# Gated linear attention levels: one head per row tile in two banks, both halves of a level in one step, q without zeros, and the third output copy ahead of the exponent

## The chip, the cores and the metric

The kernel runs on one core of one Trainium2 chip. The metric is the time of one execution on the device in microseconds. The kernel before takes 1231.93 us (median of three runs, 1231.51 to 1234.69).

## The reference, cut to what matters

The input is 16 sequences of 512 tokens with 256 features, all fp32. Each goes through a layer norm, gated linear attention, a second layer norm and a residual, then a layer norm, a two-layer feed-forward block with the weights of one of eight experts (two sequences share an expert), another layer norm and a residual. The attention has 4 heads with 64 key and 128 value features:

```python
def step(S, inp):
    qt, kt, vt, gt = inp
    S = jnp.exp(gt)[:, None] * S + kt[:, None] * vt[None, :]
    return (S, qt @ S)
...
q = (x @ Wq) ... * scale;  k = (x @ Wk);  v = (x @ Wv)
g = log_sigmoid(x @ gk_w1 @ gk_w2 + gk_b) / 16.0
o = scan(step)                                    # over 512 tokens, per head
o = o * rsqrt(mean(o * o) + EPS) * rms_w
o = o.reshape(b, t, DV) * silu(x @ Wg)
return o @ Wo
...
h = gelu(tokens @ w1[e] + b1[e]);  y = h @ w2[e] + b2[e]
```

## The kernel before, in words

The scan is done in chunks of 128 tokens. Inside a chunk the matrix of q times k with all decays between the two tokens is built in seven levels with half block sizes h = 1, 2, 4, ..., 64 (`LV`). At level i the tokens of the second half of each block of 2h tokens are multiplied with the keys of its first half; then q of the second halves is multiplied by the product of the gates of the first halves, and k of the first halves by that of the second halves (`q_update` on VectorE, L631; `k_update` on GpSimd, L1142). After seven levels q and k carry the decay to the chunk's ends, as the state needs it.

Features lie on partitions: 256 key features are two tiles (`tl`) of 128 partitions, with two heads each. q is stored block-diagonally in `qbd` (L65): [128, tl, head of the tile, 512 tokens], with zeros where the partitions belong to the other head, so that one matmul over 128 rows gives both heads side by side. A half level (`level(i, tl)`, L283) issues, for the levels 0 to 4 (`MASKED`), 16 fp32 matmuls in blocks of 32 tokens: 32 keys stationary, 2 x 16 q columns moving, the output in one of four strips of 32 partitions of bank `PL[tl]`. The compiler makes two passes (a weight load and a matmul each) of an fp32 matmul. VectorE copies the valid places by mask to `AC` (`copy_pairs`, L610). Levels 5 and 6 use blocks of 32 and 64 keys, and ScalarE copies their outputs to `Am` (`copy_blocks`, L899). The diagonal comes from `diag_rows` and `diag_columns`; `expand` (L911) puts the 32-token blocks into `Am`.

All engines run an order written out by hand in a function `run(s, j, e, B, C, A)`, called once per step. In a step of the main loop, part B is the levels and attention of sequence s, part C the feed-forward of sequence s - 1, part A the start of sequence s + 1 (layer norm, gates, k and q projections; v and output gate projections too). j is 1 for odd s. The loop has 14 steps with A, B and C; before it stand a step with A alone and one with A and B, after it one with B and C and one with C.

The level stage is a loop over 14 half levels, `step` = 2i + tl, on every engine. TensorE issues a half level and then one slice of other work (L509 to L525): `f1(m)`, six untiled matmuls of 512 columns for one of eight feature tiles of the first feed-forward layer, or `f2(c)`, 24 of 256 columns. ScalarE makes the GELU and the high part `h_hi` of each f1 slice and VectorE the low part `h_lo`. Each level waits for the q update, the k update and the copies of the level before (L294 to L300). With j = 1, GpSimd also makes the low parts of W2 in the level stage (`weight_lo`, L1175); with j = 0, ScalarE makes the high part of the next W1 at step 11 (`weight_hi`, L891, L983) and GpSimd its four low parts from step 12 on, the last two between the `rsqrt(3, c)` that end the feed-forward's layer norm.

Then comes the middle stage: x transposes, `kh` (keys to tokens), the gate matmuls `gd` and `gl`, `kp`, `qp`, `vp`, `gp` (projections of sequence n = s + 1), and per chunk c the state `st(c)`, attention `att(c)` into the one bank `PO`, the transposes `ogt(c)` and the output projection `wo(c)` (L526 to L580). `att(c)` waits until ScalarE has copied the output of chunk c - 1 out of `PO` (`o_evac`, L919, waited for at L474). ScalarE's order around the third copy is at L1014 to L1033: `o_evac(1)`, `squares(1)`, `og_hi(0)`, `v_evac(0)`, the exponent that gives the gates (L1023, with a table load), `g_evac(0)` (Silu, with a table load), `v_evac(1)`, `o_evac(2)`. VectorE writes q times scale times gates to `qg`, which shares its memory with the gates' argument `gm` (L80); ScalarE copies it from there into the two diagonal blocks of `qbd` (`q_blocks`, L948, four copies). `S` (L75) holds the state of the two heads of a tile one above the other; `att` multiplies it head by head with `qbd`.

Of the kernel before, what the change touches and what calls it, by code (L numbers as in the profile page):

```python
# [21 lines left out]
def build(nc, x_d, wq_d, wk_d, wv_d, wg_d, w1g_d, w2g_d, gkb_d, wo_d, rms_d,  # L22
# [6 lines left out]
    P = 128  # L29
# [22 lines left out]
    with ctx:  # L52
# [12 lines left out]
        qbd = sb("q_blockdiag", [P, KT, 2, T])  # L65
# [9 lines left out]
        S = sb("state", [P, KT, HV])  # L75
# [4 lines left out]
        gm = qg = sb("gate_and_q", [P, 2, T])  # L80
# [49 lines left out]
        def totals(h):  # L130
# [11 lines left out]
            pe_drow=1, pe_diag=1, pe_lv=2 * NL, pe_kt=2, pe_st=NCH - 1, pe_att=NCH, pe_ogt=NCH, pe_wo=NCH,  # L142
# [7 lines left out]
            dv_c0=KT, dv_cp=2 * MASKED, dv_qu=2 * NL, dv_st=2 * (NCH - 1) - 1, dv_og=NCH * H,  # L150
# [6 lines left out]
            ac_xhi=KT, ac_gr=1, ac_abs=KT, ac_e=1, ac_l=1, ac_a=1, ac_k=KT, ac_v=NCH, ac_g=NCH, ac_qb=2 * KT,  # L157
# [6 lines left out]
            po_p1=1, po_p2=NCH, po_p3=NCH, po_p4=NCH, po_x2=NCH, po_fin=NCH, po_tot=NL, po_ku=2 * NL,  # L164
# [14 lines left out]
        def states(c):  # L179
            return max(2 * c - 1, 0)  # L180
# [78 lines left out]
        def _(pe):  # L259
# [19 lines left out]
            def run(s, j, e, B, C, A):  # L279
# [3 lines left out]
                def level(i, tl):  # L283
                    h = LV[i]
                    if i == 0:
                        if tl == 0:
                            pe.wait_ge(sem["ac_qb"], at("ac_qb", s, 2 * KT))
                            pe.wait_ge(sem["dv_q"], at("dv_q", s, 2 * KT))
                            if C:
                                pe.wait_ge(sem["ac_o"], at("ac_o", p, NCH))  # L290
                            pe.wait_ge(sem["ac_k"], at("ac_k", s, KT))
                        if C:
                            pe.wait_ge(sem["dv_t"], at("dv_t", p, 3 + tl))
                    else:  # L294
                        pe.wait_ge(sem["dv_qu"], at("dv_qu", s, 2 * (i - 1) + tl + 1))
                        pe.wait_ge(sem["po_ku"], at("po_ku", s, 2 * (i - 1) + tl + 1))
                        if i - 1 < MASKED:
                            pe.wait_ge(sem["dv_cp"], at("dv_cp", s, 2 * (i - 1) + tl + 1))
                        else:
                            pe.wait_ge(sem["ac_cp"], at("ac_cp", s, 4 * (tl + 1)))  # L300
                    for c in range(NCH):
                        if i < MASKED:
                            for g in range(CH // BS):
                                t = slice(c * CH + BS * g, c * CH + BS * (g + 1))
                                q = qbd[:, tl, :, t].rearrange("p a (n t h) -> p a n t h", t=2, h=h)
                                last = nc.tensor.matmul(PL[tl][BS * g:BS * (g + 1), c * BS:(c + 1) * BS],  # L306
                                                        kk[:, tl, t], q[:, :, :, 1, :], start=True, stop=True)
                            continue
                        for b in range(HC // h):
                            g = h * (c % 2) + 64 * b  # L310
                            t = c * CH + 2 * h * b
                            last = nc.tensor.matmul(PL[tl][g:g + h, (c // 2) * 2 * h:(c // 2 + 1) * 2 * h],  # L312
                                                    kk[:, tl, t:t + h], qbd[:, tl, :, t + h:t + 2 * h],
                                                    start=True, stop=True)
                    last.then_inc(sem["pe_lv"], 1)

                def diag_rows():

                    for tl in range(KT):
# [40 lines left out]
                def kh(f):  # L360
                    pe.wait_ge(sem["po_ku"], at("po_ku", s, 2 * NL))
# [106 lines left out]
                def att(c):  # L468
                    pe.wait_ge(sem["ac_ex"], at("ac_ex", s, 4 * KT))
                    pe.wait_ge(sem["ac_cp"], at("ac_cp", s, 12))  # L470
                    pe.wait_ge(sem["dv_qu"], at("dv_qu", s, 2 * NL))
# [4 lines left out]
                    for hd in range(H):  # L476
                        tl, hh = hd // 2, hd % 2
                        w = slice(hd * HV, (hd + 1) * HV)
                        last = nc.tensor.matmul(PO[:, w], Am[:, tl, 2 * c + hh, :], v[:, c, w],  # L479
                                                start=True, stop=(c == 0))  # L480
                        if c:
                            last = nc.tensor.matmul(PO[:, w], qbd[:, tl, hh, c * CH:(c + 1) * CH],  # L482
                                                    S[:, tl, :], start=False, stop=True)
# [25 lines left out]
                for step in range(2 * NL):  # L509
                    if B:  # L510
                        level(step // 2, step % 2)
                        if step == 1:
                            diag_rows()
                        if step == 3:
                            diag_columns()
                        if not C and 2 <= step < 10:
                            (vp, gp)[step % 2](step // 2 - 1, s)
                    if C:
                        if step == 1:
                            x3t(0)  # L520
                            x3t(1)
# [40 lines left out]
                if V:  # L562
                    gp(1, n)
# [708 lines left out]
```

## Time and profile before

| | |
|---|---|
| median of three runs | 1231.93 us |
| profiled execution, its own time | 1233.3 us |
| its span, first to last instruction | 1231.5 us |
| PE busy | 1129.4 us (92%), 12368 matmul passes |
| PEld busy | 923.2 us (75%) |
| VectorE busy | 863.8 us (70%) |
| ScalarE busy | 813.9 us (66%) |
| GpSimd busy | 630.6 us (51%) |
| granted TensorE clock, mean; 29.6 to 30.7 us; 542.9 to 543.6 us | 0.979; 0.50; 1.00 |
| chain that ended last | PE 62%, ACT 21%, DVE 9%, issue 7% |

PE is TensorE's matmuls, PEld its weight loads, which overlap them; DVE, ACT and POOL are VectorE, ScalarE and GpSimd. An end of a matmul is modelled, so the start times say more than the lengths. In a timeline a line merges neighbouring instructions of one form, with their count, and in square brackets stands the idle time of the engine before it and who ended it. A form as `128*32 128x32` is stationary rows by columns, then the output's partitions by columns.

### The profile page before, as it was taken

How to read it: one execution, taken by the hardware profiler on the slowest of the kernel's cores; microseconds unless marked ns; L12 is line 12 of the kernel's file. 1: busy time of each engine (PE TensorE's matmuls, PEld its weight loads, DVE VectorE, ACT ScalarE, POOL GpSimd, SP SyncE). 2: the span in 40 equal slices, each digit the busy share in tenths (PEclk: the TensorE clock that was granted, in tenths of full speed). 3: DMA queues.
4: the chain of work that ended last, by engine and by line, in shares of the span. 5: the costliest groups of instructions: out<-in, count | busy, mean ns of one | idle time of the engine just before them, and what ended most of it. 6: DMA issues, size and time to landing. Idle time of an engine off the chain costs nothing.

```text
span 1231.5 us, 31412 instructions
## 1 busy us (share of the span) xinstructions
PE 1129.4 (92%) x12368; PEld 923.2 (75%) x12368; DVE 863.8 (70%) x1973; ACT 813.9 (66%) x1749; POOL 630.6 (51%) x906
## 2 busy tenths in 40 slices
PE   3799999999999999989999998999999999998967
PEld 3576878768787777878778687877878778787756
DVE  4649678585876859687685967868587684967653
ACT  5575757777577676866777575777757667586533
POOL 5437355373555544574445735547355463556541
PEclk9789999999999999999999999999999999999988
DMA  3110010100110001100011001010011000110000
GB/s 105 41 35 19 18 53 6 53 19 18 53 54 22 2 18 54 57 19 16 5 52 57 20 18 53 6 53 19 19 53 42 28 7 18 54 57 1 2 18 18
DMA packets 32145, 38.83 MB, mean 32 GB/s; under 512 B 2752, under 2 KB 29440, under 8 KB 32000
## 3 DMA queue, kind: packets, MB, share of 16 engines
q1 hardware_dynamic: 31472, 36.30, 9.0%
q8 instruction: 100, 1.64, 0.6%
q10 hardware_dynamic: 528, 0.52, 0.1%
q14 instruction: 45, 0.37, 0.1%
HBM read 28.43 MB, written 8.39 MB: 30 GB/s over the span
## 4 chain that ended last, share of the span: by engine, by line
PE 62%; ACT 21%; DVE 9%; issue 7%; POOL 1%; DMA 0%; POOLq 0%; ACTq 0%; DVEq 0%
PE ps_big L265 16%; PE ps_big L266 13%; PE ps_big L267 13%; PE ps_out L479 3%; ACT square_out L933 3%; PE ps_level L306 3%; PE ps_level L312 2%; ACT o L878 2%; PE ps_level L265 2%; DVE xT_lo L608 2%; ACT L946 2%; PE ps_out L482 2%; ACT L1010 1%; PE ps_transpose L493 1%; ACT q_times_k L1004 1%
## 5 line engine op out<-in xcount | busy, mean ns | idle before, releaser
L1151 POOL TENSOR_TENSOR k_decayed<-k_decayed,block_totals 128x256 f32<-128x256 f32 x192 | 152.2, 795 | 189.7 <-PE ps_level L306 96.0
L638 DVE TENSOR_TENSOR q_blockdiag<-q_blockdiag,block_totals 128x512 f32<-128x512 f32 x192 | 167.3, 871 | 24.9 <-PE ps_level L312 23.2
L1157 POOL TENSOR_TENSOR rstd<-mean_var,minus_half 128x1 f32<-128x1 f32 x192 | 108.6, 568 | 84.7 <-DVE mean_var L676 84.7
L265 PE MATMUL ps_big<-w_ff_hi,h_hi 128*128 128x256 f32 x512 | 150.7, 294 | 0.0
L266 PE MATMUL ps_big<-w_ff_lo,h_hi 128*128 128x256 f32 x512 | 144.8, 283 | 0.0
L267 PE MATMUL ps_big<-w_ff_hi,h_lo 128*128 128x256 f32 x512 | 144.7, 283 | 0.0
L479 PE MATMUL ps_out<-v,attn_T 128*128 128x128 f32 x512 | 99.8, 293 | 26.9 <-ACT o L878 26.9
L886 ACT ACTIVATE ps_transpose<-ps_big,ff_b_cols 128x512 f32<-128x512 f32 x128 | 84.7, 662 | 57.9 <-PE ps_big L267 55.9
L265 PE MATMUL ps_big<-xT_hi,w_ff_hi 128*128 128x512 f32 x256 | 115.1, 450 | 8.1 <-DVE xT_lo L608 7.9
L1169 POOL TENSOR_SCALAR o_rstd<-o_sumsq 128x4 f32<-128x4 f32 x64 | 12.4, 193 | 196.1 <-ACT square_out L933 196.1
L306 PEld LDWEIGHTS ps_level<-q_blockdiag,k_decayed 128*32 128x32 f32 x5120 | 56.5, 112 | 74.1 <-DVE q_blockdiag L638 41.8
L265 PE MATMUL ps_big<-w_vg_hi,xT_hi 128*128 128x512 f32 x256 | 109.7, 429 | 0.7
L1181 POOL TENSOR_TENSOR w_ff_lo<-w_raw,w_ff_hi 128x512 fp32r<-128x512 f32 x64 | 96.1, 1503 | 19.0 <-ACT w_ff_hi L878 18.8
L479 PEld LDWEIGHTS ps_out<-v,attn_T 128*128 128x128 f32 x512 | 76.5, 198 | 37.9 <-issue 37.9
L265 PEld LDWEIGHTS ps_big<-w_ff_hi,h_hi 128*128 128x128 f32 x512 | 97.8, 191 | 6.5 <-issue 5.1
L266 PE MATMUL ps_big<-xT_lo,w_ff_hi 128*128 128x512 f32 x256 | 102.2, 399 | 0.4 <-issue 0.4
L267 PE MATMUL ps_big<-xT_hi,w_ff_lo 128*128 128x512 f32 x256 | 102.1, 399 | 0.0
L643 DVE TENSOR_TENSOR h_lo<-ps_transpose,h_hi 128x512 fp32r<-128x512 f32 x128 | 87.4, 683 | 19.6 <-ACT h_hi L878 19.0
L266 PE MATMUL ps_big<-w_vg_lo,xT_hi 128*128 128x512 f32 x256 | 101.1, 395 | 0.0
L267 PE MATMUL ps_big<-w_vg_hi,xT_lo 128*128 128x512 f32 x256 | 101.0, 395 | 0.0
L267 PEld LDWEIGHTS ps_big<-w_ff_hi,h_lo 128*128 128x128 f32 x512 | 97.9, 191 | 0.0
L266 PEld LDWEIGHTS ps_big<-w_ff_lo,h_hi 128*128 128x128 f32 x512 | 97.9, 191 | 0.0
(132 smaller groups left out, 3205.7 us busy)
## 6 DMA issues: line engine op xcount, KB each, us to landing
w_raw<-L_ffn_w SPq DMA_DIRECT2D x16, 1024.0 KB, 6.0
out<-y SPq DMA_DIRECT2D x16, 512.0 KB, 3.2
x_in<-L_attn_x SPq DMA_DIRECT2D x15, 512.0 KB, 3.8
ff_b_rows<-L_ffn_b SPq DMA_DIRECT2D x8, 128.0 KB, 2.1
x_in<-L_attn_x ACTq DMA_DIRECT2D x1, 512.0 KB, 4.4
w_raw<-L_attn_Wv SPq DMA_DIRECT2D x1, 512.0 KB, 5.3
w_raw<-L_attn_Wg SPq DMA_DIRECT2D x1, 512.0 KB, 6.4
y<-L_attn_Wo SPq DMA_DIRECT2D x1, 512.0 KB, 7.4
```

The source lines that it names most:

```text
L265: nc.tensor.matmul(out, ah, bh, start=(first and i == 0), stop=False)
L266: nc.tensor.matmul(out, ah, bl, start=False, stop=False)
L267: last = nc.tensor.matmul(out, al, bh, start=False, stop=(final and i == n - 1))
L306: last = nc.tensor.matmul(PL[tl][BS * g:BS * (g + 1), c * BS:(c + 1) * BS], kk[:, tl, t], q[:, :, :, 1, :], start=True, stop=True)
L479: last = nc.tensor.matmul(PO[:, w], Am[:, tl, 2 * c + hh, :], v[:, c, w], start=True, stop=(c == 0))
L638: nc.vector.tensor_tensor(q, q, t.to_broadcast([P, 2, T // (2 * h), h]), ALU.mult)\
L643: nc.vector.tensor_tensor(h_lo[:, m, :], PT[m % 2][:, :], h_hi[:, m, :].bitcast(F32), ALU.subtract).then_inc(sem["dv_hlo"], 1)
L886: nc.scalar.activation(PT[m % 2][:, :], PB[m % 2][:, :], ACT.Gelu_apprx_tanh, bias=b1s[:, m:m + 1]).then_inc(sem["ac_gelu"], 1)
L933: nc.scalar.activation(junk[:, w], o[:, c % 2, hd * HV:(hd + 1) * HV], ACT.Square, accum_out=ssq[:, c * H + hd:c * H + hd + 1]).then_inc(s ...
L1151: nc.gpsimd.tensor_tensor(k, k, t.to_broadcast([P, n, h]), ALU.mult)\
L1157: nc.gpsimd.tensor_tensor(rs[:, k, c:c + 1], mv[:, k, c, 1:2], mhalf[:, 0:1], ALU.pow)\
L1181: nc.gpsimd.tensor_tensor(flat[1], raw[:, part * w:(part + 1) * w], flat[0].bitcast(F32), ALU.subtract).then_inc(sem[name], 1)
```

## The change

q is stored once, as `qs` [128, tl, 512]. A matmul of a level takes the 64 partitions of one head as its rows, so that the heads of a tile are two row tiles; head 0 of both tiles writes to `PL[0]`, head 1 to `PL[1]`. Levels 0 to 4 now have 64 matmuls of 16 columns where 2 x 16 of 32 columns stood; level 5 has 32 of 32 columns for 2 x 8 of 64; level 6 has 16 of 64 columns for 2 x 4 of 128. A level is one step: one `q_update` and one `k_update` over both tiles, both `copy_pairs` behind the whole level. Between two levels stand two slices of f1, or of f2 behind level 5. The state becomes block-diagonal (`S` [128, tl, 2, 128]) and is updated head by head; `att` multiplies it for both heads at once. VectorE writes q straight to its place and `q_blocks` is gone. `o_evac(2)` stands behind `v_evac(0)`, ahead of the exponent; `squares(2)` and `og_hi(1)` come ahead of `g_evac(0)`; `wo(1)` comes ahead of `gp(1)`. `weight_hi(0)` moves from step 11 of 14 to behind the level loop and the low parts of W1 with it.

```diff
-        qbd = sb("q_blockdiag", [P, KT, 2, T])
+        qs = sb("q", [P, KT, T])
-        S = sb("state", [P, KT, HV])
+        S = sb("state_blockdiag", [P, KT, 2, HV])
-        gm = qg = sb("gate_and_q", [P, 2, T])
+        gm = sb("gate", [P, 2, T])
...
-                def level(i, tl):
+                def level(i):
...
+                    for tl in range(KT):
+                        for c in range(NCH):
+                            if i < MASKED:
+                                for g in range(CH // BS):
+                                    t = slice(c * CH + BS * g, c * CH + BS * (g + 1))
+                                    w = (tl * NCH + c) * (BS // 2)
+                                    for hh in range(2):
+                                        r = slice(hh * HK, (hh + 1) * HK)
+                                        q = qs[r, tl, t].rearrange("p (n t h) -> p n t h", t=2, h=h)
+                                        last = nc.tensor.matmul(PL[hh][BS * g:BS * (g + 1), w:w + BS // 2],
+                                                                kk[r, tl, t], q[:, :, 1, :], start=True, stop=True)
+                                continue
+                            for b in range(HC // h):
+                                g = h * (c % 2) + 64 * b
+                                t = c * CH + 2 * h * b
+                                w = (tl * 2 + c // 2) * h
+                                for hh in range(2):
+                                    r = slice(hh * HK, (hh + 1) * HK)
+                                    last = nc.tensor.matmul(PL[hh][g:g + h, w:w + h], kk[r, tl, t:t + h],
+                                                            qs[r, tl, t + h:t + 2 * h], start=True, stop=True)
...
+                    for tl in range(KT):
                         if c:
+                            nc.tensor.matmul(PO[:, 2 * tl * HV:2 * (tl + 1) * HV], qs[:, tl, c * CH:(c + 1) * CH],
+                                             S[:, tl, :, :], start=True, stop=False)
...
+                for i in range(NL):
                     if B:
+                        level(i)
+                        if i == 0:
                             diag_rows()
+                    if C and i == 0:
+                        x3t(0)
+                        x3t(1)
+                    if B and i == 1:
+                        diag_columns()
+                    if B and not C and 1 <= i <= NCH:
+                        vp(i - 1, s)
+                        gp(i - 1, s)
+                    if C and 1 <= i < 5:
+                        f1(2 * i - 2)
+                        f1(2 * i - 1)
+                    if C and i == 5:
+                        f2(0)
+                        f2(1)
+                    if C and i == 6:
+                        f2(2)
...
                     att(3)
+                    wo(1)
                 if V:
                     gp(1, n)
                 if B:
-                    wo(1)
                     ogt(2)
...
+                def q_update(i):
                     h = LV[i]
+                    q = qs[:, :, :].rearrange("p k (n t h) -> p k n t h", t=2, h=h)[:, :, :, 1, :]
+                    t = totals(h).rearrange("p k (n t a) -> p k n t a", t=2, a=1)[:, :, :, 0, :]
+                    nc.vector.tensor_tensor(q, q, t.to_broadcast([P, KT, T // (2 * h), h]), ALU.mult)\
                         .then_inc(sem["dv_qu"], 1)
+                def absorb(i):
+                    dve.wait_ge(sem["pe_lv"], at("pe_lv", s, i + 1))
+                    if i < MASKED:
+                        copy_pairs(i, 0)
+                        copy_pairs(i, 1)
+                    if i == 0:
+                        dve.wait_ge(sem["po_tot"], at("po_tot", s, NL))
+                    q_update(i)
+                    if i == 2:
+                        copy_diag(0)
+                        copy_diag(1)
...
+                    for hh in range(2):
+                        r = slice(hh * HK, (hh + 1) * HK)
+                        if c == 0:
+                            nc.vector.tensor_copy(S[r, :, hh, :], PS[r, 0:KT * HV].rearrange("p (k v) -> p k v", k=KT))\
+                                .then_inc(sem["dv_st"], 1)
+                            continue
...
+                for i in range(NL):
+                    if C and 2 <= i < 6:
+                        if i > 2:
+                            h_lo_part(2 * i - 5)
+                        h_lo_part(2 * i - 4)
+                    if i == 6:
+                        if C:
+                            h_lo_part(FT - 1)
+                        if A:
                             ln1_stats()
                             ln1_aggregate()
+                        if C:
+                            ln4(0)
...
+                    if B:
+                        absorb(i)
...
-                def q_blocks(tl):
...
-                    for hh in range(2):
-                        r = slice(hh * HK, (hh + 1) * HK)
-                        copy(qbd[r, tl, hh, :], qg[r, tl, :], "ac_qb")
...
+                if A and j == 0:
+                    weight_hi(0, 0 if not C else e + 1)
...
-                    if V:
-                        v_evac(0, n)
+                if V:
+                    v_evac(0, n)
+                if B:
+                    o_evac(2)
+                if A:
                     act.wait_ge(sem["dv_gsub"], at("dv_gsub", n, 1))
                     nc.scalar.activation(ga[:, :, :], gm[:, :, :], ACT.Exp, scale=1.0 / GATE_NORM)\
                         .then_inc(sem["ac_a"], 1)
+                if B:
+                    squares(2)
+                    og_hi(1)
                 if V:
                     g_evac(0, n)
                     v_evac(1, n)
                 if B:
-                    o_evac(2)
-                    squares(2)
-                    og_hi(1)
                     o_evac(3)
                     squares(3)
...
+                for i in range(NL):
                     if B:
+                        k_update(i)
+                    if C and j == 1 and 1 <= i < 5:
+                        weight_lo(1, i - 1, e)
+                    if A and i == 5:
                         pool.wait_ge(sem["dv_ln1"], at("dv_ln1", n, 2 * NCH))
...
+                if split_w1:
+                    weight_lo(0, 0, next_e)
+                    weight_lo(0, 1, next_e)
```

## Rows read from the trace of the kernel before

**Rows 1.** Windows: us, PE PEld DVE ACT POOL busy (instructions), PEclk, DMA share, GB/s

```profile
542.90:574.70 31.80, 29.63 (x515) 23.46 (x515) 27.15 (x55) 21.66 (x42) 20.98 (x22) 1.00 0.05 15
```

**Rows 2.** Waits of TensorE, whole run: us in total, times, longest

```profile
PE ps_out L479 <- ACT o L878: 26.9, 15, 1.9
```

**Rows 3.** Groups by line: busy us, mean ns | idle before, releaser

```profile
L638 DVE TENSOR_TENSOR q_blockdiag<-q_blockdiag,block_totals 128x512 f32<-128x512 f32 x192 | 167.3, 871 | 24.9 <-PE ps_level L312 23.2
L1151 POOL TENSOR_TENSOR k_decayed<-k_decayed,block_totals 128x256 f32<-128x256 f32 x192 | 152.2, 795 | 189.7 <-PE ps_level L306 96.0 <-PE ps_level L312 92.4
L619 DVE COPY_PREDICATED attn_blocks<-level_masks,ps_level 128x128 f32<-128x128 uint32 x160 | 56.8, 355 | 19.0 <-PE ps_level L306 16.6
```

**Rows 4.** Timeline of TensorE, one half level and one slice: start, length, xcount

```profile
558.11 0.46 PE L306 MATMUL ps_level<-q_blockdiag,k_decayed 128*32 128x32 f32 x32
558.50 0.50 PE L265 MATMUL ps_big<-xT_hi,w_ff_hi 128*128 128x512 f32 x1
558.84 0.39 PE L266 MATMUL ps_big<-xT_lo,w_ff_hi 128*128 128x512 f32 x1
...
559.76 0.40 PE L267 MATMUL ps_big<-xT_hi,w_ff_lo 128*128 128x512 f32 x1
560.09 0.46 PE L306 MATMUL ps_level<-q_blockdiag,k_decayed 128*32 128x32 f32 x32
```

**Rows 5.** Timeline of TensorE, level 0 to the first f1 slice

```profile
542.94 0.75 PE L306 MATMUL ps_level<-q_blockdiag,k_decayed 128*32 128x32 f32 x63
543.50 0.29 PE L321 MATMUL ps_out<-q_times_k,head_sum 128*32 128x128 f32 x1
...
547.61 0.50 PE L265 MATMUL ps_big<-xT_hi,w_ff_hi 128*128 128x512 f32 x1 [0.64 <-DVE xT_lo L608]
```

**Rows 6.** Timelines of TensorE's weight loads in short windows

```profile
549.21 0.19 PEld L306 LDWEIGHTS ps_level<-q_blockdiag,k_decayed 128*32 128x32 f32 x12 [0.36 <-issue]
...
543.22 0.29 PEld L306 LDWEIGHTS ps_level<-q_blockdiag,k_decayed 128*32 128x32 f32 x22
...
29.69 0.95 PEld L306 LDWEIGHTS ps_level<-q_blockdiag,k_decayed 128*32 128x32 f32 x64 [7.56 <-ACT q_blockdiag L878]
```

**Rows 7.** Timeline of TensorE, starts of f1, f2, level 6 and transposes

```profile
564.38 0.39 PE L265 MATMUL ps_big<-w_ff_hi,h_hi 128*128 128x256 f32 x1
...
567.46 0.66 PE L312 MATMUL ps_level<-q_blockdiag,k_decayed 128*64 128x128 f32 x8
568.04 0.39 PE L265 MATMUL ps_big<-w_ff_hi,h_hi 128*128 128x256 f32 x1
...
574.66 1.04 PE L275 MATMUL ps_transpose<-ident,x_normed 128*128 128x128 f32 x8
...
621.02 0.50 PE L265 MATMUL ps_big<-xT_hi,w_ff_hi 128*128 128x512 f32 x1 [0.48 <-DVE xT_lo L608]
...
636.78 0.39 PE L265 MATMUL ps_big<-w_ff_hi,h_hi 128*128 128x256 f32 x1
```

**Rows 8.** Timelines of ScalarE and TensorE around the third output copy

```profile
519.21 0.57 ACT L878 ACTIVATE v<-ps_big 128x512 f32<-128x512 f32 x1
...
524.44 0.60 ACT L878 ACTIVATE o<-ps_out 128x512 f32<-128x512 f32 x1
...
525.29 0.46 PE L479 MATMUL ps_out<-v,attn_T 128*128 128x128 f32 x2 [1.78 <-ACT o L878]
```

**Rows 9.** Timelines of four engines where new weights are split

```profile
496.77 1.92 ACT L878 ACTIVATE w_ff_hi<-w_raw 128x2048 fp32r<-128x2048 f32 x1
...
504.01 1.28 POOL L1181 TENSOR_TENSOR w_ff_lo<-w_raw,w_ff_hi 128x512 fp32r<-128x512 f32 x1
...
507.43 0.69 DVE L736 TENSOR_TENSOR gate_lowrank<-ps_level,gate_lowrank 32x512 fp32r<-32x512 f32 x1
...
509.45 0.62 PE L409 MATMUL ps_level<-gate_lowrank,w_gate_up 128*128 128x512 f32 x2
```

**Rows 10.** Timeline of VectorE, last q of the first sequence

```profile
27.54 0.68 DVE L756 SCALAR_TENSOR_TENSOR gate_and_q<-ps_big,gates 128x512 f32<-128x512 f32 x1
```

More of the change, by code:

```diff
@@ L179, in states @@
         def states(c):
-            return max(2 * c - 1, 0)
+            return max(4 * c - 2, 0)
         def at(name, b, c):
@@ L297, in level @@
                         if i - 1 < MASKED:
-                            pe.wait_ge(sem["dv_cp"], at("dv_cp", s, 2 * (i - 1) + tl + 1))
+                            pe.wait_ge(sem["dv_cp"], at("dv_cp", s, 2 * i))
                         else:
[L300 to L314, printed above, removed]
@@ L475, in att @@
                         pe.wait_ge(sem["dv_st"], at("dv_st", s, states(c)))
[L476 to L480, printed above, removed]
-                        if c:
-                            last = nc.tensor.matmul(PO[:, w], qbd[:, tl, hh, c * CH:(c + 1) * CH],
-                                                    S[:, tl, :], start=False, stop=True)
+                    for tl in range(KT):
+                        if c:
+                            nc.tensor.matmul(PO[:, 2 * tl * HV:2 * (tl + 1) * HV], qs[:, tl, c * CH:(c + 1) * CH],
+                                             S[:, tl, :, :], start=True, stop=False)
+                        for hh in range(2):
+                            w = slice((2 * tl + hh) * HV, (2 * tl + hh + 1) * HV)
+                            last = nc.tensor.matmul(PO[:, w], Am[:, tl, 2 * c + hh, :], v[:, c, w],
+                                                    start=(c == 0), stop=(c == 0 or hh == 1))
                     last.then_inc(sem["pe_att"], 1)
@@ L787, in run @@
                                 const_lo(0)
+                    if B:
+                        absorb(i)
+                    if C and i == 0:
+                        for kt in range(KT):
+                            lo_part(xT_lo[:, kt, :], xT_hi[:, kt, :], PT[kt][:, :], "ac_x3hi", p, kt + 1, "dv_x3lo")
+                if C:
+                    ln4(1)
                 if A:
@@ L1196, in run @@
                             late_constants()
-                    if split_w1 and step >= 12:
-                        weight_lo(0, step - 12, next_e)
+                if split_w1:
+                    weight_lo(0, 0, next_e)
+                    weight_lo(0, 1, next_e)
                 if C:
```

179 lines of the change are left out of this document (63 added, 116 removed).

## The prediction

> **What bounds the kernel now.** I read the time by stage first, then who TensorE waits for, then its timeline stretch by stretch. One step of the main loop takes 73.6 us and has two parts: a level stage (31.8 us from the first level to the first x transpose) and a middle stage (state, attention, projections, 41.8 us). In the level stage TensorE is busy 29.63 of 31.80 us, VectorE 27.15, ScalarE 21.66, GpSimd 20.98 [rows 1]: TensorE bounds it and VectorE is close behind. Over the whole run TensorE's largest single wait is for ScalarE's copy of the attention output, 26.9 us in 15 waits of about 1.8 us [rows 2]. So there are two places to earn: the TensorE work of the levels, and that wait.
>
> **The change, part by part.**
>
> *Levels on TensorE.* Per step there were 14 half levels, each followed by one slice of other work. A half of levels 0 to 4 is 32 passes (16 fp32 matmuls, two passes each). A half level starts at 558.11, the next untiled matmul at 558.50, and the next half level at 560.09: 0.39 for the half, 1.59 for the rest. Four untiled matmuls take 0.92 (558.84 to 559.76), so 0.23 each and 1.40 for the six of a slice; 0.19 is lost in changing over [rows 4]. After the change a level is one block of 64 matmuls, 128 passes of half the columns, in eight tiles (two row halves by four column strips), then two slices. What do 128 passes cost? Rows 6 give the pace of weight loads, one per pass: 12 start within 0.08 us at the beginning of a level (length 0.19 less the 0.11 of the last load), 6.9 ns each; further in, 22 start within 0.18 us, 8.2 ns each; in the first sequence, at half the granted clock (0.50 there), 64 take 0.95, less some 0.16 for the last, 12.3 ns. Had the array's streaming set the warm pace, it would be half of the cold one, about 6.2; it is 8.2. So I read the warm pace as one of issuing instructions, which halving the columns does not quicken. 128 passes at 8.2 ns are 1.05; with 0.14 for the end (0.39 less 32 passes at 7.8, an estimate between the two paces) a level costs 1.19. Bounds: 0.56 if eight tiles run their passes as 64 passes run now in four (542.94 to 543.50 [rows 5]), and 3.4 if a change of row half cost what a change-over does (0.14 for each of 16 groups of eight passes, on top). I take 1.19, the value of the pace row.
>
> One page of the Trainium skill speaks against this part: "TensorEngine Tiling (Array Packing)", Instruction Overhead, says a matmul of one column takes as long as one of 60 and tells not to take the tiling factor from a dimension that is already small; here it is taken from 32 columns. Rows 6 neither show nor exclude that for 16 columns; by it the array would hold each of the eight tiles 16 times 25 ns, 0.40 us, less than the issue pace, so it would leave the sum as it is. The page "TensorE: Matmul & The Clock Gate", section "Wait — 56ns, not 53.3ns?", gives a floor of some 25 ns from start to start; read as one floor for the whole array it would make 3.2 us of a level, but the 8.2 ns of rows 6 refute that reading, so it can hold only within a tile.
>
> Sum of the stage, first slice to last. (a) Between two levels: before 2 x 1.98 = 3.96, after 2 x 1.40 + 0.19 + 1.19 = 4.18. (b) From the first slice of f1 to the first of f2: before 15.76 (621.02 to 636.78) in a step without the next weights' low parts on GpSimd, 16.77 (547.61 to 564.38) in one with them, where VectorE and GpSimd slow each other [rows 5, 7]. After: eight slices 11.2, levels 2 to 4 at 1.38, level 5 (64 passes, 0.53 + 0.14 + 0.1), 0.1: 16.2. That is +0.4 and -0.6. (c) From the first f2 to the x transposes: before 10.28 (564.38 to 574.66), three slices with three change-overs and two halves of level 6 [rows 7]. After, one level 6 of 32 passes, 64 columns, four tiles: 8 passes per tile at 0.055 + 0.14 = 0.58 for two halves at 0.58 (567.46 to 568.04; less 0.14 that is 0.11 for each of the four passes of a strip, of 128 columns, so 0.055 for 64), and one change-over of 0.2 fewer: about -0.75. (d) From level 0 to the first f1: before 4.67 (542.94 to 547.61). Level 0 takes 1.05 instead of 0.56 [rows 5]; both q halves are then updated by one instruction of 512 elements where two of 512 stood (half of what the block-diagonal form multiplied was zeros; 871 ns each, [rows 3]), so VectorE starts 0.5 later and works 1.1 less. TensorE next waits for the k update, two halves at 0.8 alone, slower beside VectorE, so one instruction of about 2.0 (an estimate), until 3.2; level 1, then f1 at 4.5 to 4.7: no change. Together -0.35 in the one kind of step and -1.3 in the other.
>
> *Cover.* The copies, q and k updates of a level now have to end within two slices, 2.8 us: VectorE needs 2 x 0.36 + 0.9 to 1.0, GpSimd 2 x 0.8 = 1.6 [rows 3]. The first piece of low part in VectorE's queue stands ahead of them and is ready when the level ends. Slack about 0.8 us on VectorE; gone, each 0.1 beyond it would cost 0.1 at up to four levels. VectorE gives up 7 x 0.87 = 6.1 us per step, and ScalarE its four q copies, in a stretch where nothing waits for them except at the start of the run.
>
> *State.* The block-diagonal state is updated by 2, 4 and 4 instructions of 64 partitions instead of 1, 2 and 2, about +0.3 and +0.6 us, with 1 us or more before attention asks for it. Attention streams the same columns. Nothing.
>
> *Third output copy.* Before, it begins at 524.44, behind two table loads, the exponent, gate and v copy that follow the v copy of 519.21; TensorE stands 1.78 until 525.29 [rows 8]. Now it comes right behind that first v copy, as soon as attention 2 ends near 520, and is done by 520.5. TensorE reaches attention 3 at 523.5 without a stop. Next in line is the output projection 1, moved ahead of the gate projection: it needs the low part of ogT, ready at 525.4 when attention 3 ends at 525.3. Later the chain og, ogT, projection 3 keeps nearly the whole shift. I take 1.6 in each of 14 steps and 1.7 in the first.
>
> *The next weights.* In every second step ScalarE's high part of W1 (496.77, 1.92 long) moves from ahead of level 6 to behind its copies, so it ends about 0.5 after the x transposes begin (501.05 then). GpSimd's four low parts at 1.28 [rows 9] with three rstd (0.55) and an output add (0.7) among them take 7.4 more: 509.0. VectorE's low-rank part, in order behind the norm that waits for these, begins at 509.4 instead of 507.43, and TensorE's gate matmul (509.45) can start at 510.15: +0.7 in seven steps [rows 9].
>
> *Ends.* The first level waits for ScalarE's block-diagonal copies until 29.69 (a wait of 7.56 [rows 6]); q itself is ready at 28.2 (27.54 + 0.68) [rows 10], and the W_o constants leave VectorE's way too: -3. The last step with levels: -1.3.
>
> Sum: seven pairs of steps at (-0.35 - 1.6 + 0.7) + (-1.3 - 1.6) = -4.15 are -29; first step's copy -1.7, ends -4.3: -35. The profiled execution took 1233.3 (span 1231.5), which gives 1198.3; the median of the runs, 1231.93, is 1.4 lower, so I forecast 1197.
>
> **The rivals.**
>
> *A. The row halves really overlap and nothing limits issue.* A level costs 0.56. For it: the 6.9 ns at the start of a level; against: 8.2 further in. Saves 0.63 at levels 2 to 4, 0.25 at level 5, up to 0.5 at level 0, some 2.6 in 15 steps: 1197 - 39 = 1158.
>
> *B. Slower: row halves of one column strip take turns.* If a pass must end before the other half of its strip is loaded, 32 passes queue per strip. At 0.055 each, the pace of 64 columns, a level is 1.76 + 0.14 = 1.90: +0.7 at four to five levels and as much again over levels 5 and 6, +3.3 in 15 steps, 1197 + 50 = 1247. It decides from a level of about 1.75, where 15 x 4 x 0.55 eats the 35 earned. For it: no row before uses less than 128 rows. Against: column strips do overlap (a pass starts every 8.2 ns) [rows 6], and nothing marks the row halves as different.
>
> *C. The shift in the middle is given back.* ScalarE is full from 508 to 527, and behind the copy wait og and the ogT copies. If they bind, 1.6 shrinks to 0.3: +20, 1217. The same figure comes if whole levels now wait for VectorE and GpSimd by 0.35 at four levels.
>
> *D. Little changes:* B in half and C together, 1232.
>
> **How the numbers follow.** Forecast 0.50, A 0.17, C 0.19, B 0.10, D 0.04. A measurement of this kernel tells 0.3%, 3.7 us. Forecast, A and C are faster: 0.86; same 0.04; slower 0.10. The range leaves out B and D: 1156 (A with a little more) to 1226 (C with a level of 1.3). The likeliest case alone is 1185 to 1208, a level of 1.0 to 1.35.
>
> **What would show it.** The block of a middle level: 128 passes in 1.05 to 1.2 us, and 4.2 from level to level. TensorE's wait for the output copy gone from the list (26.9). The first level near 28.3. The gate matmul in steps with new weights behind a wait for VectorE. VectorE's q updates half as many, of about 0.9 to 1.0. Wrong: a level of 0.6 (A) or 1.8 (B); a wait for o or ogT_lo before the projections (C); waits of k or q at levels 2 to 5.

## The result, and the profile after

| | kernel before | changed kernel |
|---|---|---|
| median of the runs made together, us | 1233.31 (1231.51 to 1234.97, 4 runs) | 1293.2 (1290.84 to 1302.21, 4 runs) |
| ratio, with 95% interval | | 1.0499 (1.0446 to 1.0553) |
| profiled execution / its span, us | 1233.3 / 1231.5 | 1293.6 / 1291.6 |
| mean granted TensorE clock | 0.979 | 0.952 |
| TensorE instructions (matmul passes and weight loads) | 24,736 | 36,128 |

The change costs 60 us where 35 were to be earned, a gap of 95 us. First the page of the profile after: the busy times with instruction counts, the clock row (tenths, 40 slices), the queue that brings instructions (transfers, MB, share of 16 engines), and the chain of waits by engine. Before, the queue made 100 transfers, and the chain had ACT 21% and issue 7%.

```profile
PE 1160.3 (90%) x18064; PEld 972.7 (75%) x18064; DVE 839.9 (65%) x1941; ACT 772.9 (60%) x1685; POOL 590.5 (46%) x794
PEclk8799999999999898999989999898999999899998
q8 instruction: 144, 2.36, 0.8%
PE 62%; ACT 16%; issue 9%; DVE 8%; POOL 4%; DMA 0%; POOLq 0%; ACTq 0%; DVEq 0%
```

TensorE executes 46% more instructions, and they are what q8 carries: with the semaphore waits in the same stream the trace has 36,917 of them after and 25,621 before, and over 144 and 100 transfers that is 256 each; a transfer is 16.4 KB (2.36 MB over 144). In the chain ScalarE lost five points, with its output copy gone, and issue gained two. Next TensorE's waits, in the list of waits (us in total, times, longest):

```profile
PE ps_level L308 <- issue: 42.6, 31, 3.7
...
PE ps_transpose L275 <- issue: 10.6, 6, 4.0
PE ps_level L265 <- DVE ogT_lo L618: 9.1, 30, 1.4
PE ps_level L415 <- DVE gate_lowrank L760: 8.2, 7, 1.2
PE ps_level L308 <- DVE q L646: 6.4, 9, 1.6
...
PE ps_level L308 <- DVE q L782: 6.0, 1, 6.0
PE ps_big L265 <- issue: 5.9, 4, 2.1
...
PE ps_out L333 <- issue: 2.3, 1, 2.3
```

The wait for ScalarE's output copy [rows 2] is gone, as forecast. In its place stands a name that the prediction did not have: "issue", idle time in which TensorE waits for nothing that the profile shows. All its entries of that kind sum to 63.8 us in 46 waits; before they were 1.8 us in 5.

Now TensorE's timeline where nothing is amiss (start, length, operation), and then twice where it is (the window cuts off the first row's beginning, level 0 starts at 645.20):

```profile
586.51 1.26 PE L308 MATMUL ps_level<-q,k_decayed 64*32 64x16 f32 x128
587.71 0.48 PE L265 MATMUL ps_big<-xT_hi,w_ff_hi 128*128 128x512 f32 x1
590.65 1.26 PE L308 MATMUL ps_level<-q,k_decayed 64*32 64x16 f32 x128
```

```profile
645.82 0.65 PE L308 MATMUL ps_level<-q,k_decayed 64*32 64x16 f32 x54
646.39 0.64 PE L327 MATMUL ps_out<-q_times_k,head_sum 128*32 128x128 f32 x16
646.97 1.09 PE L275 MATMUL ps_transpose<-ident,x_normed 128*128 128x128 f32 x8
651.74 1.45 PE L308 MATMUL ps_level<-q,k_decayed 64*32 64x16 f32 x128 [3.67 <-issue]
655.48 0.47 PE L333 MATMUL ps_out<-ident,o 128*128 128x128 f32 x1 [2.30 <-issue]
```

A middle level takes 1.20 us (586.51 to 587.71) and the slot from level to level 4.14. But between level 0 and level 1 of the next step TensorE stands 3.67 us, and 2.30 again behind level 1. The instruction queue in windows of the same stretch: the first 0.2 us, then the next 3.5, then 0.2, then 3.8 without a transfer, then 0.2 (only windows with a transfer have the row).

```profile
q8 instruction: 1, 0.02, 36.9%
...
q8 instruction: 1, 0.02, 40.0%
...
q8 instruction: 1, 0.02, 31.1%
```

The three transfers begin at 649.20, 652.88 and 656.89; the first two idle times end at 651.74 and 655.48, which is 2.54 and 2.60 after a transfer began. Over the whole trace 44 of the 46 "issue" waits stand in this stage (the other two, of under 0.3 us, in the first middle stage), and each of the 44 ends 2.2 to 3.2 us after such a beginning, and no two transfers begin closer than 3.29 us. At one place (809.58 to 813.53, a stand of 3.95) the previous transfer was 22.6 us back: the refill, which began at 811.00, came 1.4 us after TensorE had stopped.

The place of the waits settles what they are. A wait can cut a level in two, where the kernel has no semaphore to wait for:

```profile
339.72 0.24 PE L308 MATMUL ps_level<-q,k_decayed 64*32 64x16 f32 x6 [0.63 <-DVE q L646]
342.48 1.34 PE L308 MATMUL ps_level<-q,k_decayed 64*32 64x16 f32 x122 [2.52 <-issue]
```

If one counts TensorE's instructions (weight loads, passes and semaphore waits) from the start of the trace, the number before each of these 44 waits is 193 more than a multiple of 256, without an exception: TensorE stops where one transfer ends and the next has not come. The same count says how little is held: when a transfer begins, at most 289 instructions of those before it are left, and none at six of the 144.

The clock goes with it. In the table by windows (window, length, busy times, granted clock in tenths of one behind the engines, DMA share, GB/s), the level behind the first idle time and a stretch behind the second:

```profile
651.70:652.90 1.20, 1.17 (x123) 1.17 (x126) 0.00 (x0) 0.00 (x0) 0.00 (x0) 0.50 0.07 14
656.00:660.00 4.00, 4.00 (x10) 3.06 (x10) 0.00 (x0) 1.40 (x2) 0.00 (x0) 0.50 0.02 4
660.00:664.80 4.80, 4.80 (x143) 3.64 (x141) 3.48 (x7) 3.49 (x6) 1.16 (x1) 0.97 0.02 3
```

TensorE had been idle for 3.67 and 2.30 us and then worked at 0.50, the 1.2 GHz level, until about 660.3 (0.97 in the last window). In the steady part of the run such stretches sum to about 78 us after, against 10 before. Projections at half the clock take up to twice as long, so 68 us more of them cost at most 34 us. With 62.0 us more of "issue" that is up to 96, against a gap of 95; but part of those stretches is idle time and counted already. A second estimate: with neither such waits nor half clock the way from level 0 to the gate-down projection would take 34.99 us (its four parts, under *What failed*, as they measured in steps that had neither); less their "issue" time, the 14 of the main loop are 25 us longer in sum. So some 25 us for the clock, and 87 of the 95 together.

### The profile page after: what moved, and what is told of

The parts are those of the page before. It is cut to its first block, busy times and chain, and to the rows that moved or that the text cites. A ratio compares the mean times of both kernels' runs of the same rounds, so it can differ in the third digit from the quotient of the medians.

```text
span 1291.6 us, 42213 instructions
## 1 busy us (share of the span) xinstructions
PE 1160.3 (90%) x18064; PEld 972.7 (75%) x18064; DVE 839.9 (65%) x1941; ACT 772.9 (60%) x1685; POOL 590.5 (46%) x794
## 3 DMA queue, kind: packets, MB, share of 16 engines
q8 instruction: 144, 2.36, 0.8%
## 4 chain that ended last, share of the span: by engine, by line
PE 62%; ACT 16%; issue 9%; DVE 8%; POOL 4%; DMA 0%; POOLq 0%; ACTq 0%; DVEq 0%
PE ps_big L265 14%; PE ps_big L266 13%; PE ps_big L267 13%; PE ps_level L308 8%; ACT square_out L960 3%; POOL w_ff_lo L1197 3%; PE ps_out L488 2%; PE ps_out L484 2%; PE ps_level L317 2%; ACT L1044 1%; PE ps_state L469 1%; PE ps_transpose L275 1%; ACT ogT_hi L904 1%; DVE o L689 1%; ACT gates L1044 1%
## 5 line engine op out<-in xcount | busy, mean ns | idle before, releaser
L1167 POOL TENSOR_TENSOR k_decayed<-k_decayed,block_totals 128x512 f32<-128x512 f32 x96 | 120.8, 1258 | 296.8 <-PE ps_level L308 225.6
L308 PEld LDWEIGHTS ps_level<-q,k_decayed 64*32 64x32 f32 x10240 | 97.0, 109 | 85.3 <-issue 69.8
L308 PE MATMUL ps_level<-q,k_decayed 64*32 64x16 f32 x10240 | 107.8, 191 | 55.1 <-issue 42.6
L265 PE MATMUL ps_big<-xT_hi,w_ff_hi 128*128 128x512 f32 x256 | 119.1, 465 | 5.9 <-issue 4.4
L646 DVE TENSOR_TENSOR q<-q,block_totals 128x512 f32<-128x512 f32 x96 | 104.2, 1085 | 21.0 <-PE ps_level L317 20.3
L266 PE MATMUL ps_big<-xT_lo,w_ff_hi 128*128 128x512 f32 x256 | 110.2, 430 | 1.4 <-issue 1.3
L267 PE MATMUL ps_big<-xT_hi,w_ff_lo 128*128 128x512 f32 x256 | 109.9, 429 | 0.6 <-issue 0.6
L265 PE MATMUL ps_big<-w_vg_hi,xT_hi 128*128 128x512 f32 x256 | 105.9, 414 | 2.0 <-issue 1.5
L629 DVE COPY_PREDICATED attn_blocks<-level_masks,ps_level 128x128 f32<-128x128 uint32 x160 | 47.7, 367 | 85.1 <-PE ps_level L308 85.0
L689 DVE SCALAR_TENSOR_TENSOR o<-o,o_rstd,out_gate 128x128 f32<-128x128 f32 x256 | 79.5, 371 | 16.8 <-POOL o_rstd L1188 16.6
```

What stands on the lines that cost most here:

```text
L265: nc.tensor.matmul(out, ah, bh, start=(first and i == 0), stop=False)
L266: nc.tensor.matmul(out, ah, bl, start=False, stop=False)
L267: last = nc.tensor.matmul(out, al, bh, start=False, stop=(final and i == n - 1))
L308: last = nc.tensor.matmul(PL[hh][BS * g:BS * (g + 1), w:w + BS // 2], kk[r, tl, t], q[:, :, 1, :], start=True, stop=True)
L629: nc.vector.copy_predicated(dst, m.to_broadcast([P, KT * NCH, BS // (2 * h), h]), src)\
L646: nc.vector.tensor_tensor(q, q, t.to_broadcast([P, KT, T // (2 * h), h]), ALU.mult)\
```

## The experiments

Two theories stood against each other. **F (supply):** TensorE runs out of instructions, because a level now takes 256 of them in 1.2 us, and about 560 stand between the start of level 0 and the first slice of f1 (level 0, diagonal rows, transposes, level 1: 256 + 32 + 16 + 256), while a transfer of 256 comes at most every 3.3 to 3.7 us. **R (row tiles):** the small tiles are slow in themselves, whoever supplies them (rival B's family). In each diff below the lines are those of the matmul loops or of the order of the work.

**e1_one_tile**: half of the level matmuls left out.

```diff
                     for tl in range(KT):
+                        if i < MASKED and tl == 1:
+                            continue
```

> The changed kernel with the matmuls of levels 0 to 4 issued for the first of the two feature tiles only (64 passes a level instead of 128, still alternating between the two row halves; the second tile's blocks are left out). Theory F (TensorE runs out of fetched instructions: its 36,000 instructions come in 144 transfers of 256, never less than 3.3 us apart, and levels 0 and 1 with what lies between are some 560 in under 5 us): the idle that TensorE shows as 'issue', about 63 us in the changed kernel, falls below 10, the mean clock goes back to 0.975, a level takes 0.60, and the time is 1165 to 1180. Theory R (alternating row halves of a strip cause the stalls): half of the alternations are left, so half of the issue idle, 25 to 35 us, and 1215 to 1240.

Measured 1186.8 us, ratio 0.9636 (0.96 to 0.9672), clock 0.976, 104 transfers on the instruction queue, "issue" 9.1 us in 7 waits. The head of its list of waits, where "issue" does not stand any more:

```profile
PE ps_transpose L275 <- DVE x_normed L720: 11.6, 2, 9.7
PE ps_level L310 <- DVE q L648: 9.5, 15, 0.6
```

Some 106 us go with 64 passes fewer at each of five levels in 16 steps; by the pace of 8.2 ns [rows 6] those are 0.53 us each, 42 in all. Much more is gone than the passes' own time, which speaks for F; R had its numbers 30 us higher. The time is 7 above F's range.

**e2_one_row**: both heads from the same 64 rows, so that no pass changes row half; same count.

```diff
-                                        r = slice(hh * HK, (hh + 1) * HK)
+                                        r = slice(0, HK)
```

> The changed kernel with all matmuls of levels 0 to 4 taking the first 64 partitions (the first head twice, into both banks; the second head of each tile is left out there). As many instructions as in the changed kernel, no change of row half. Theory F: nothing changes, issue idle 50 to 75 us, 1285 to 1300. Theory R: issue idle under 10, 1195 to 1215.

Measured 1293.55 us, ratio 1.0503 (1.0461 to 1.0544), clock 0.947.

```profile
PE ps_level L308 <- issue: 27.2, 23, 2.9
...
PE ps_transpose L275 <- issue: 9.5, 6, 3.3
```

A level in its timeline:

```profile
585.82 1.41 PE L308 MATMUL ps_level<-q,k_decayed 64*32 64x16 f32 x128
587.16 0.50 PE L265 MATMUL ps_big<-xT_hi,w_ff_hi 128*128 128x512 f32 x1
```

The total of "issue" is 45.8 us in 39 waits, a little under what F named, and the time is that of the changed kernel. A level takes 1.34 us in these four tiles (585.82 to 587.16), 0.14 more than in eight: to change the row half costs nothing, it gains. So R is refuted, and rival B with it. That the two times are equal is in part chance: 80 levels at 0.14 are 11 us more of matmuls, beside 18 us less of "issue".

**e3_twice**: the kernel before, with each block-diagonal matmul of levels 0 to 4 issued twice: the instruction count of the change (17,488 passes against 18,064) without its row tiles, its columns or its order.

```diff
                                 q = qbd[:, tl, :, t].rearrange("p a (n t h) -> p a n t h", t=2, h=h)
+                                nc.tensor.matmul(PL[tl][BS * g:BS * (g + 1), c * BS:(c + 1) * BS],
+                                                 kk[:, tl, t], q[:, :, :, 1, :], start=True, stop=True)
```

> The kernel before with every matmul of levels 0 to 4 issued twice: 128 rows, block-diagonal q, the old order, but as many level passes as the changed kernel. The array's work alone: 32 more passes at 8.2 ns in 10 half levels of 16 sequences, 42 us, so 1275. Theory F: issue idle appears, mostly around levels 0 and 1, 20 to 60 us, and the clock falls below 0.97: 1295 to 1330. Theory R: no issue idle, 1270 to 1280.

Measured 1299.87 us, ratio 1.0554 (1.0514 to 1.0594), 140 transfers, clock 0.977.

```profile
PE ps_level L308 <- issue: 15.1, 12, 3.0
PE ps_level L306 <- issue: 10.6, 10, 2.8
...
PE ps_out L323 <- issue: 5.3, 3, 1.9
```

Waits of up to 3.0 us with the name "issue" (32.0 us in 27) appear in a kernel that has nothing of the change but its count, and 26 of the 27 stand on the same boundary of 256. The time proves less than the waits do: a half level takes 0.79 us here, where it took 0.39, so 160 of them are 64 us of passes, and not the 42 in the expectation. The clock did not fall below 0.97 as I had expected; the idle times are fewer and shorter, which may be why.

**e10_first_two**: the changed kernel with the second tile left out at levels 0 and 1 only.

```diff
                     for tl in range(KT):
+                        if i < 2 and tl == 1:
+                            continue
```

> The changed kernel with the second feature tile's matmuls left out at levels 0 and 1 only (64 passes there, 128 at levels 2 to 4). Theory F: the burst of some 560 instructions before the first f1 shrinks to 300, and with it the large stalls: issue idle 15 to 30 us, all at levels 2 to 5, 1230 to 1250. If the stalls come from the levels with 128 passes in equal parts: issue idle some 40, 1255 to 1265.

Measured 1240.51 us, ratio 1.0048 (1.0024 to 1.0072), 128 transfers, clock 0.973; "issue" 30.6 us, at the upper edge of what F named, most of it at one line:

```profile
PE ps_level L310 <- issue: 24.2, 24, 2.4
```

These 24 waits of about 1 us lie mostly at levels 2 to 5. So there are two shortages: the burst at levels 0 and 1, which makes most of the long ones, and the steady pace behind it, where a slot of 4.14 us takes 280 instructions, one refill per 3.8 us. In the bursts refills do come as close as that. Where TensorE waits at levels 2 to 5, they mostly begin some 5 us apart; why they come no sooner there is not shown.

**e9_slow**: the changed kernel with every slice of f1 computed twice, which lengthens the slots of levels 2 to 5 and leaves levels 0 and 1 as they are.

```diff
-                    three(PB[m % 2][:, :], [(W1[0][:, kt, w], W1[1][:, kt, w]) for kt in range(KT)],
-                          [(xT_hi[:, kt, :], xT_lo[:, kt, :]) for kt in range(KT)]).then_inc(sem["pe_f1"], 1)
+                    for again in range(2):
+                        last = three(PB[m % 2][:, :], [(W1[0][:, kt, w], W1[1][:, kt, w]) for kt in range(KT)],
+                                     [(xT_hi[:, kt, :], xT_lo[:, kt, :]) for kt in range(KT)])
+                    last.then_inc(sem["pe_f1"], 1)
```

> The changed kernel with each f1 slice computed twice in a row (12 untiled matmuls instead of 6; the second overwrites the first with the same values). More instructions in all, but 256 + 48 per 7 us between two levels instead of 256 + 24 per 4.2. The array's work alone: 16 x 8 x 1.40 = 179 us more. Theory F as a matter of demand per time (a chunk of 256 per some 3.7 us can be had): the stalls at levels 2 to 5, 15 to 25 us of the 64, go, those around levels 0 and 1 stay: issue idle 35 to 48, time 1440 to 1462. If every chunk boundary that falls into a level costs its stall whatever the demand: issue idle 60 or more, time 1468 or more.

Measured 1413.09 us, ratio 1.1435 (1.1369 to 1.1501), clock 0.975.

```profile
PE ps_level L308 <- issue: 21.3, 12, 3.0
```

"issue" in all is 27.0 us and the time 27 us below F's range: F had the place of the waits right and their size too large. In the main loop none of it stands later than 9 us behind the start of a level 0: levels 2 to 5 have no idle time of that kind once a slot is longer. The extra slices are 16 x 8 x 1.40 = 179 us of TensorE work, yet the time grew by 120 (1413 less 1293): some 59 us were given back, by "issue" waits that went (63.8 to 27.0) and by a clock of 0.975 for 0.952.

**e5_fill**: the changed kernel with V and gate projection 3 moved from the end of the middle to behind level 0, so that these two stand between the two bursts.

```diff
+                        if B:
+                            vp(3, s)
+                            gp(3, s)
...
-                    vp(3, n)
-                    gp(3, n)
```

(ScalarE's `v_evac(3)` and `g_evac(3)` move with them, as in the next two fills.)

> The changed kernel with the last two projections of a middle stage (vp(3), gp(3): 2.8 us of TensorE with 24 instructions) moved behind level 0 and diag_rows of the next level stage, ahead of the x3 transposes; as many instructions in all. Theory F: they give the fetch time where it is short, between levels 0 and 1; issue idle falls from 63 to 20 to 40, time 1250 to 1270. If the stalls hang on the levels themselves and not on the demand per time: no change of the issue idle, 1285 to 1295.

Measured 1272.39 us, ratio 1.0321 (1.0279 to 1.0363), clock 0.968.

```profile
PE ps_level L308 <- issue: 41.0, 32, 3.7
```

"issue" is 53.4 us in 42 waits, where I had expected 20 to 40, and the time is 2 us above the range: a miss of F in size. A level alone asks for 256 instructions in 1.2 us, so almost every level crosses a refill, and other work between two levels shortens the wait only when the refill happens to be early. What starts a transfer, and at what number of instructions left, stays open.

**e4_mid**: the kernel before with the change's order in the middle stage alone.

```diff
-                if A:
-                    if V:
-                        v_evac(0, n)
+                if V:
+                    v_evac(0, n)
+                if B:
+                    o_evac(2)
+                if A:
                     act.wait_ge(sem["dv_gsub"], at("dv_gsub", n, 1))
...
+                if B:
+                    squares(2)
+                    og_hi(1)
                 if V:
                     g_evac(0, n)
                     v_evac(1, n)
                 if B:
-                    o_evac(2)
-                    squares(2)
-                    og_hi(1)
```

(and `wo(1)` ahead of `gp(1)` on TensorE.)

> The kernel before with only the middle stage of the change: third output copy behind the v copy and ahead of the exponent, second output projection ahead of the gate projection. TensorE's 26.9 us of waits for the output copy go, and 1.7 us of each of 15 middle stages with them in both kinds of step: 1203 to 1210. If the chain of og and ogT gives it back: above 1220. If the lateness of the next weights' low parts, and not the middle stage, made the changed kernel's second kind of step gain only 0.35, both kinds gain alike here.

Measured 1204.86 us, ratio 0.9779 (0.9751 to 0.9808): 26 us from the order of the middle stage alone.

```profile
PE ps_level L306 <- DVE q_blockdiag L638: 18.2, 24, 2.1
...
PE ps_level L265 <- DVE ogT_lo L608: 9.0, 30, 1.4
```

The 26.9 us of ACT o are gone; 9.0 of ogT_lo are new. From the gate-down projection to the next first level both kinds of step take 36.04 us, for 37.57 before: 1.53 less each.

**e6_mid_fill**: e4_mid with the same move of V and gate projection 3 as in e5_fill.

> The kernel with the new middle stage alone (1204.9) and the same move of vp(3) and gp(3) behind level 0. They cover the waits of levels 1 and of the first f1 for VectorE, some 0.65 and 0.5 us a step: 14 x 0.7 to 1.2 us less, 1188 to 1196. If ScalarE's copies of them delay the high parts of x3: 1200 to 1210.

Measured 1200.76 us, ratio 0.9738 (0.9722 to 0.9754): 4 us for a hoped-for 9 to 17, a miss.

```profile
PE ps_level L306 <- ACT q_blockdiag L879: 16.7, 16, 7.1
...
PE ps_level L306 <- DVE q_blockdiag L639: 8.9, 9, 2.1
```

The wait for VectorE's block-diagonal q at level 1 shrank by 9.3 us (18.2 to 8.9), and the first level now waits for ScalarE's half of it: 16.7 against 7.1 before. With the two projections out of the end of the middle, ScalarE's copies there had lost their cover.

**e7_pair**: e4_mid with the change's steps, but on the old tiles: block-diagonal q on 128 rows, both 32-pass halves of a level together, then two slices.

```diff
-                for step in range(2 * NL):
+                for i in range(NL):
                     if B:
-                        level(step // 2, step % 2)
+                        level(i, 0)
+                        level(i, 1)
...
+                    if C and 1 <= i < 5:
+                        f1(2 * i - 2)
+                        f1(2 * i - 1)
```

> The new middle stage, and both halves of a level in one step as in the change, but with the block-diagonal q, 128 rows and 64 passes a level as before. Theory F: 64 passes a level leave the fetch in time, issue idle under 10. TensorE's level with two slices would be 3.55 us, VectorE's 2 x 0.36 + 2 x 0.9 to 1.0 + 2 x 0.68 = 4.0, against 3.96 before: VectorE bounds the levels, 1195 to 1215. If grouping the halves by itself brings stalls: above 1230.

Measured 1186.1 us, ratio 0.962 (0.9604 to 0.9636), 100 transfers, clock 0.985, "issue" 1.2 us; better than expected. TensorE's timeline at a middle level:

```profile
600.75 0.76 PE L306 MATMUL ps_level<-q_blockdiag,k_decayed 128*32 128x32 f32 x64
601.44 0.50 PE L265 MATMUL ps_big<-xT_hi,w_ff_hi 128*128 128x512 f32 x1
...
604.41 0.76 PE L306 MATMUL ps_level<-q_blockdiag,k_decayed 128*32 128x32 f32 x64
```

A whole level takes 0.69 us in 64 passes where the change takes 1.20 in 128, and a slot 3.66, for 4.14 in the change and 3.96 before. VectorE still updates the zeros, two instructions a level of 0.91 us, and the slots stay at 3.66 behind that.

**e8_pair_fill**: e7_pair with the move of e5_fill, the version to which the others pointed.

> Both: halves in one step with block-diagonal q, and vp(3), gp(3) behind level 0, with the new middle stage. 0.7 to 1.2 us a step less than the halves in one step without the move: 1180 to 1200.

Measured 1182.01 us (1181.76 and 1182.25), ratio 0.9588 (0.9569 to 0.9607), "issue" 0.5 us, clock 0.986. It is the fastest of all kernels here that compute the reference, 51 us below the kernel before and 111 below the changed one.

## Why the prediction was wrong

**What held.** The pace of issue: level 1.19 forecast, 1.20 measured; slot 4.18 forecast, 4.14 measured. Those are the terms of (a), and rival A (0.56) and rival B (1.90) fall by them, B also by e2_one_row. The first level starts at 28.83 for the 28.3 of *Ends* (29.69 before, [rows 6]). The middle stage: 37.57 became 35.81 in one kind of step, -1.76 for the -1.6 of *Third output copy*. In the other kind it became 37.23: -0.34 for -0.9, because the gate matmul waits for VectorE's low-rank part for 1.17 us (8.2 in 7 waits) where *The next weights* had 0.7. e4_mid, which leaves the weights in place, has no such wait and 36.04 in both kinds; nor has e7_pair, where only the high part is still inside the level loop and the low parts have moved. That points at the move of the high part. The ogT_lo waits of e4_mid (9.0 us in 30) are rival C's mechanism at a size that left the gain standing.

**What failed.** The sum of the level stage. Its paragraphs (a) to (d) priced 128 passes at 8.2 ns as if the next instruction were always there, and *Cover* asked only whether VectorE and GpSimd would keep up. The rows read before could not refute that: there a half slot of 1.98 us [rows 4] took 76 instructions, one refill per 6.7 us, and "issue" was 1.8 us in the whole run. What was mis-sized is a term that the sum did not have: 62 us of idle time for instructions, and up to 34 us of work at half the clock behind it. It shows in the stages. From the first level to the gate-down projection a step took 36.0 or 34.8 us before and 38.4 to 45.0 after, where -0.35 and -1.3 had been forecast; with the second tile left out (e1_one_tile) it is 33.3 (once 34.5) in one kind and 32.7 to 36.5 in the other.

The terms that the sum did have held where nothing waits for instructions at the full clock: (b), forecast 16.2, took 16.15 in the one such step of e10_first_two; (c) took 9.55 for 10.27, -0.72 against -0.75. Only (d), from level 0 to the first f1, was short: 4.9 to 5.1 in such steps of e9_slow (mean 4.98), for 4.5 to 4.7. With the 4.31 from the x transposes to the gate-down projection they are the 34.99 used above.

**Was it shown?** The count alone brings the waits (e3_twice); half the count takes nearly all of them away (e1_one_tile); a second row half costs nothing (e2_one_row); burst and steady pace can be switched off apart (e10_first_two, e9_slow); the waits end 2.2 to 3.2 us behind a transfer's start, and in the changed kernel all of them stand on a boundary of 256 instructions. The share of the lost clock was not isolated: 34 us is a bound from the stretches at 0.50, 25 an estimate, and e3_twice has "issue" waits with hardly any loss of clock.

**Where the forecast's 35 us were.** All of it, and more, was to be had: 26 us by the order of the middle stage (e4_mid, ratio 0.9779), another 1.6% by one step per level (e7_pair, 0.962 over 0.9779 is 0.984), without a single instruction more. The part of the change that doubled the passes to spare VectorE its zeros bought little: TensorE's waits for VectorE's q at a level fell from 18.0 us to 6.4, where e7_pair, with the zeros, has 14.6. It cost more than the rest earned.

## What to carry to other kernels

Price a tiled matmul in instructions as well as in array time: count passes and weight loads per microsecond over the densest few microseconds, and set them beside what the instruction queue has brought in any trace, here 256 in 3.3 to 3.7 us at best. Read "issue" idle of TensorE together with the instruction queue's transfers; if idle times end a like time behind a transfer, and stand at multiples of its instructions, the cure is fewer instructions (wider tiles, even with zeros in them); another order took away only 10 of 64 us here (e5_fill). And when a change bundles a reorder with a new tiling, weigh and run each alone: here one was worth 2.2% and hid under the other's loss.

## What the runs showed of the hardware

- TensorE's instructions come in transfers of 16.4 KB, 256 instructions, never begun closer than 3.29 us. At most 289 are left when the next transfer of the changed kernel begins. When TensorE has run dry, work resumes 2.2 to 3.2 us after the transfer begins, and the whole stand is up to 4.0 us.
- Halving the columns hardly quickens small passes: 64 of 32 columns in four tiles take 0.69 us (600.75 to 601.44 in e7_pair), 64 of 16 columns in eight tiles 0.66 (e1_one_tile), 128 of 16 columns 1.20 in eight tiles and 1.34 in four (e2_one_row).
- In the changed kernel idle times of 1 to 4 us inside busy stretches were followed, 15 times, by a granted clock of 0.50 for 3 to 10 us; in the run as a whole 0.952 for 0.979. In e3_twice, with 27 idle times of up to 3.0 us, there were 5 such stretches, and the mean was 0.977. What decides between them is not shown.
